# A fused mixing and MLP kernel on one Trainium2 core: LayerNorm 2 with tokens on partitions, first denominators on GpSimd, weights' low parts on VectorE, first fold behind the second slot

## The reference, cut to what matters

```python
def _layernorm(x, axis=-1, eps=1e-05):
    m = jnp.mean(x, axis=axis, keepdims=True)
    v = jnp.var(x, axis=axis, keepdims=True)
    return (x - m) / jnp.sqrt(v + eps)

# _wkv, a scan over the 128 tokens of a sequence, k = layernorm(x), v = ctx:
y = (A * p + E * vt) / (A * q + E)
return ((A2 * p + E2 * vt, A2 * q + E2, no2), y)

# ffn:
x = fwht(x * SU_ug) / SCALE
x_up = x @ W_up.T * (Wscale_ug[:INTER] * SCALE)
x_gate = x @ W_gate.T * (Wscale_ug[INTER:] * SCALE)
x = jax.nn.silu(x_gate) * x_up
x = fwht(x * SU_dp) / SCALE
x = x @ W_down.T * (Wscale_dp * SCALE)

# the whole:
x = x + jnp.tanh(g_xattn[0]) * wkv(w, u, _layernorm(x), ctx)
x = x + jnp.tanh(g_ffn[0]) * ffn(_layernorm(x), ...)
```

## Time and profile before

| | us |
|---|---|
| median of 3 runs | 110.72 |
| lowest and highest | 109.65 and 111.17 |
| the profiled execution | 110.77 |
| its span in the profile | 109.0 |

### The profile page before, as it was taken

The page is one execution under the profiler, slowest core; times in us unless marked ns, Lnnn a source line. Parts: engine busy times, 40 slices in busy tenths (PEclk is TensorE's granted clock), DMA queues, the critical chain, the costliest instruction groups (busy, mean ns, idle before and its releaser), DMA issues.

```text
span 109.0 us, 2031 instructions
## 1 busy us (share of the span) xinstructions
PE 102.0 (94%) x728; PEld 92.4 (85%) x728; DVE 69.7 (64%) x146; ACT 68.1 (63%) x153; POOL 61.2 (56%) x73
## 2 busy tenths in 40 slices
PE   6999999798999999978999999699999999999990
PEld 5787797477667999968999989699999999999980
DVE  0399987599999995798998259932277221134211
ACT  4099969889929899925337995555975532442400
POOL 7026995996995994149996246355207243234400
PEclk9999999999999999999999999999999999999998
DMA  1899999200000000000000000020000200000202
...
DMA packets 2893, 7.70 MB, mean 71 GB/s; under 512 B 321, under 2 KB 706, under 8 KB 2754
## 3 DMA queue, kind: packets, MB, share of 16 engines
...
HBM read 6.51 MB, written 1.05 MB: 69 GB/s over the span
## 4 chain that ended last, share of the span: by engine, by line
PE 59%; ACT 14%; DVE 14%; issue 9%; DVEq 0%; POOL 0%; ACTq 0%; POOLq 0%
PE UG L960 24%; PE VB L833 9%; PE OD L998 5%; PE VB L998 3%; PE FX L998 3%; PE KZ L998 3%; ACT L558 2%; PE FX L923 2%; ACT L561 2%; DVE DEN L720 2%; PE FX L877 2%; DVE SQ L664 2%; PE OD L890 2%; PE VB L890 2%; PE KZ L890 2%
## 5 line engine op out<-in xcount | busy, mean ns | idle before, releaser
L478 POOL TENSOR_TENSOR HL<-H,HH 128x256 fp32r<-128x256 f32 x32 | 26.0, 817 | 30.0 <-ACT HH L617 29.9
L810 DVE SCALAR_TENSOR_TENSOR H<-S,ALPHA,UG 128x256 f32<-128x256 f32 x32 | 15.0, 476 | 17.5 <-ACT S L626 17.4
L626 ACT ACTIVATE S<-UG,HI 128x256 f32<-128x256 f32 x32 | 14.8, 467 | 14.6 <-PE UG L960 14.6
L960 PE MATMUL UG<-FH,WTH 128*128 128x256 f32 x128 | 21.8, 293 | 0.8 <-DVE H L810 0.7
L617 ACT ACTIVATE HH<-H 128x256 fp32r<-128x256 f32 x32 | 13.2, 411 | 12.3 <-DVE H L810 12.2
L960 PE MATMUL UG<-FL,WTH 128*128 128x256 f32 x128 | 20.2, 280 | 0.5 <-DVE FL L781 0.5
L960 PE MATMUL UG<-FH,WTL 128*128 128x256 f32 x128 | 20.1, 279 | 0.0
L960 PEld LDWEIGHTS UG<-FH,WTH 128*128 128x128 f32 x128 | 17.6, 189 | 2.4 <-issue 1.2
L960 PEld LDWEIGHTS UG<-FL,WTH 128*128 128x128 f32 x128 | 17.2, 189 | 0.7 <-DVE FL L781 0.7
L960 PEld LDWEIGHTS UG<-FH,WTL 128*128 128x128 f32 x128 | 17.2, 188 | 0.0
L833 PE MATMUL VB<-ONES 128*128 128x256 f32 x32 | 9.9, 470 | 1.0 <-POOL ONES L432 1.0
...
## 6 DMA issues: line engine op xcount, KB each, us to landing
...
```

What stands on the lines that cost most here:

```text
L478: pool.tensor_tensor(HL[:, q % JT, 0:n], ring(H, q), HH[:, q % JT, 0:n].bitcast(F32), ALU.subtract).then_inc(h_lo, 1)
L626: act.activation(ring(S, q), gate_part(q), ACT.Silu, scale=VT[:, V_SGATE + j:V_SGATE + j + 1]).then_inc(silu_ready, 1)
L810: dve.scalar_tensor_tensor(out=ring(H, q), in0=ring(S, q), scalar=ALPHA[:, j:j + 1], in1=up_part(q), op0=ALU.mult, op1=ALU.mult).then_inc( ...
L960: return pe.matmul(dst.rearrange("p (g n) -> p g n", n=GT), w[:, m, j, t, :], f[:, chunks, t, :], start=start, stop=stop, skip_group_check ...
```

## The change

LayerNorm 2: `ones` now uses the squares as the stationary operand and one column of 1/C as the moving one, so the variances stand with tokens on partitions (128x2). `ve2` (VectorE, 128x2) adds eps, `rstd2` is a power of -0.5 on GpSimd (128x2), and the new TensorE stage `spread` transposes the broadcast result into VB. ScalarE copies FX to FN (`f_kept`), and `f_scaled` is a `tensor_tensor` of FN and VB. `root` is gone, as are the Ln and Exp of `rstd2` and GpSimd's `sum`.

Mixing, chunk 0: `mix_den` runs on GpSimd; for it, ScalarE makes a second exponential with another bias (`weighted`, tile EW). The load of the Ln and Exp table moves from `setup` to behind `center`.

Weights: `w_rest` is gone. `w_lo` 0 to 3 run on VectorE, from PSUM.

Order: the first fold `m` 0 moves from ahead of slot 0 to behind slot 1, `keys` 2 from there to behind slot 2, `warm_ug` is gone, `fwht`, `ones` and the exp blocks sit later, LAG is 7.

```diff
-LAG = 6
+LAG = 7
 PE_STAGES = {
-    -1: [("warm", 9), ("keys", 0), ("warm", 5), ("center", 0), ("w", 0), ("warm", 2), ("x_part", 0), ("w", 1), ("w_rest", 0), ("keys", 1), ("w", 2),
-        ("w_rest", 1), ("w", 3), ("y_part", 0), ("w_rest", 2), ("ones", 0), ("w_rest", 3), ("m", 0), ("warm_ug", 2), ("keys", 2)],
-    1: [("m", 1)],
-    2: [("m", 2)],
-    3: [("m", 3), ("fwht", 1)],
-    4: [("keys", 3), ("ones", 1)],
-    9: [("fwht", 2)],
-    12: [("ones", 2)],
-    17: [("fwht", 3)],
-    19: [("ones", 3)],
+    -1: [("warm", 9), ("keys", 0), ("warm", 5), ("center", 0), ("w", 0), ("warm", 2), ("x_part", 0), ("w", 1), ("y_part", 0), ("keys", 1),
+        ("ones", 0), ("w", 2), ("w", 3), ("spread", 0)],
+    1: [("m", 0)],
+    2: [("keys", 2), ("m", 1)],
+    3: [("m", 2)],
+    4: [("fwht", 1)],
+    5: [("m", 3), ("ones", 1)],
+    6: [("spread", 1)],
+    8: [("keys", 3)],
+    12: [("fwht", 2)],
+    13: [("ones", 2)],
+    14: [("spread", 2)],
+    19: [("fwht", 3)],
+    20: [("ones", 3)],
+    21: [("spread", 3)],
 }
 ACT_STAGES = {
+    -1: [("setup", 0), ("own", 0), ("signs", 0), ("decay", 0), ("keys", 0), ("weighted", 0), ("ratio", 0), ("center", 0), ("log_table", 0), ("recip", 0),
+        ("w_hi", 0), ("minus", 1), ("norm1", 1), ("w_hi", 1), ("square", 0), ("f_kept", 0), ("keys", 1), ("minus", 2), ("w_hi", 2), ("w_hi", 3), ("f_hi", 0), ("w_hi", 4), ("norm1", 2),
+        ("w_hi", 5), ("w_hi", 6), ("recip", 1), ("m_hi", 0), ("w_hi", 7), ("keys", 2)],
+    0: [("m_hi", 1), ("x_hi", 1)],
+    3: [("m_hi", 2)],
+    4: [("square", 1), ("f_kept", 1)],
+    5: [("m_hi", 3)],
+    6: [("f_hi", 1)],
+    8: [("exp_block", (("recip", 2), ("keys", 3)))],
+    9: [("x_hi", 2)],
+    12: [("square", 2), ("f_kept", 2)],
+    14: [("f_hi", 2), ("exp_block", (("recip", 3),))],
+    16: [("x_hi", 3)],
+    19: [("square", 3), ("f_kept", 3)],
+    21: [("f_hi", 3)],
 }
 DVE_STAGES = {
+    -1: [("stats1", 0), ("setup_rows", 0), ("norm1", 0), ("setup_shift", 0), ("stats1", 1), ("outs", 0), ("scan_a", 0),
+        ("av", 0), ("scan_av", 0), ("mix_num", 0), ("estimate", 0), ("newton", 0), ("w_lo", 0), ("w_lo", 1), ("stats1", 2), ("ve2", 0), ("stats1", 3),
+        ("f_scaled", 0), ("f_lo", 0), ("scan_a", 1), ("mix_den", 1), ("w_lo", 2), ("w_lo", 3), ("av", 1), ("m_lo", 0), ("scan_av", 1),
+        ("mix_num", 1), ("estimate", 1), ("newton", 1)],
+    0: [("x1", 1), ("m_lo", 1), ("x_lo", 1)],
+    2: [("scan_a", 2)],
+    3: [("m_lo", 2), ("mix_den", 2)],
+    4: [("ve2", 1)],
+    5: [("scan_av", 2), ("m_lo", 3)],
+    6: [("f_scaled", 1), ("f_lo", 1), ("mix_num", 2)],
+    8: [("estimate", 2), ("newton", 2), ("x1", 2)],
...
 }
 POOL_STAGES = {
+    -1: [("rstd1", 0), ("rstd1", 1), ("mix_den", 0), ("fly", 0), ("error", 0), ("fly", 1), ("fly", 2), ("fly", 3), ("rstd2", 0), ("fly", 6),
+        ("rstd1", 2), ("rstd1", 3), ("fly", 4), ("fly", 5), ("fly", 7), ("error", 1), ("w_lo", 4), ("w_lo", 5), ("av", 2)],
+    0: [("w_lo", 6)],
+    1: [("w_lo", 7)],
+    3: [("rstd2", 1)],
+    5: [("norm1", 3)],
+    7: [("error", 2), ("av", 3)],
...
 }
...
+                elif name == "mix_den":
+
+                    pool.wait_ge(weighted, 1)
+                    pool.wait_ge(scanned_a, 2)
+                    pool.tensor_tensor(lanes(DEN[:, 0, :, :, :]), lanes(EW[:, :, :, :]), lanes(states(SQ)), ALU.add).then_inc(den_ready, 1)
+                elif name == "rstd2":
+
+                    pool.wait_ge(half, 1)
+                    pool.wait_ge(ve2, g + 1)
+                    pool.tensor_tensor(RS2[:, :], VE2[:, :], NHALF[:, :], ALU.pow).then_inc(rstd2, 1)
...
-                elif name == "rstd2":
-
-                    act.wait_ge(v_full, g + 1)
-                    if g == 0:
-                        act.wait_ge(eps_set, 1)
-                    act.activation(RR[:, :], VB[:, 0:GT], ACT.Ln, bias=EPSC[:, 0:1]).then_inc(log_ready, 1)
-                    act.wait_ge(log_ready, g + 1)
+                elif name == "f_kept":
+
+                    act.wait_ge(f_full, g + 1)
                     if g:
-                        act.wait_ge(e_ready, 3 * g)
-                    act.activation(RR[:, :], RR[:, :], ACT.Exp, scale=-0.5).then_inc(rr_ready, 1)
+                        act.wait_ge(f_hi, CT * g)
+                        act.wait_ge(f_lo, g)
+                    act.activation(FN[:, :, :], FX[:, :].rearrange("p (t n) -> p t n", t=CT), ACT.Copy).then_inc(f_kept, 1)
...
+                elif name == "ve2":
+                    dve.wait_ge(v_full, g + 1)
+                    dve.tensor_scalar(VE2[:, :], VB[:, 0:GB], EPS * C, None, ALU.add).then_inc(ve2, 1)
                 elif name == "f_scaled":
-                    dve.wait_ge(e_ready, 3 * g + 3)
...
+                    dve.wait_ge(spread, g + 1)
+                    dve.wait_ge(f_kept, g + 1)
+                    for t in range(CT):
+                        dve.tensor_tensor(FN[:, t, :], FN[:, t, :], VB[:, GT:2 * GT], ALU.mult).then_inc(f_scaled, 1)
...
+                    for t in range(CT):
+                        pe.wait_ge(squared, t + 1 if g == 0 else CT + g)
+                        for b in range(GB):
+                            i = pe.matmul(VB[:, b:b + 1], FSQ[:, t, b * P:(b + 1) * P], ONES[:, 0:1], start=(t == b == 0), stop=(t == CT - 1), skip_group_check=True)
                     i.then_inc(v_full, 1)
+                elif name == "spread":
+
+                    pe.wait_ge(const_in, 16)
+                    pe.wait_ge(rstd2, g + 1)
+                    for b in range(GB):
+                        i = pe.matmul(VB[:, GT + b * P:GT + (b + 1) * P], RS2[:, b:b + 1].broadcast_to([P, P]), IDENT, is_transpose=True,
+                                      start=(b == 0), stop=(b == GB - 1), skip_group_check=True)
+                    i.then_inc(spread, 1)
```

More of the change, by code:

```diff
@@ L70 @@
+    0: [("m_hi", 1), ("x_hi", 1)],
[10 more added lines that the diff above has]
+    21: [("f_hi", 3)],
 }
 DVE_STAGES = {
-    -1: [("stats1", 0), ("setup_rows", 0), ("norm1", 0), ("setup_shift", 0), ("stats1", 1), ("outs", 0), ("scan_a", 0), ("mix_den", 0),
-        ("av", 0), ("scan_av", 0), ("mix_num", 0), ("estimate", 0), ("newton", 0), ("stats1", 2), ("stats1", 3),
-        ("scan_a", 1), ("root", 0), ("f_scaled", 0), ("mix_den", 1), ("f_lo", 0), ("m_lo", 0), ("av", 1), ("scan_av", 1), ("mix_num", 1),
-        ("estimate", 1), ("newton", 1), ("x1", 1)],
@@ new lines @@
+    0: [("x1", 1), ("m_lo", 1), ("x_lo", 1)],
[5 more added lines that the diff above has]
+    8: [("estimate", 2), ("newton", 2), ("x1", 2)],
+    9: [("x_lo", 2), ("scan_a", 3)],
+    11: [("mix_den", 3)],
+    12: [("ve2", 2)],
+    13: [("scan_av", 3)],
+    14: [("f_scaled", 2), ("f_lo", 2), ("mix_num", 3), ("estimate", 3), ("newton", 3)],
+    15: [("x1", 3)],
@@ L89 @@
+    16: [("x_lo", 3)],
+    19: [("ve2", 3)],
+    21: [("f_scaled", 3), ("f_lo", 3)],
 }
 POOL_STAGES = {
-    -1: [("rstd1", 0), ("rstd1", 1), ("fly", 0), ("fly", 1), ("fly", 2), ("error", 0), ("fly", 3), ("fly", 6), ("rstd1", 2), ("fly", 4), ("rstd1", 3),
-        ("fly", 5), ("fly", 7), ("w_lo", 4), ("error", 1), ("w_lo", 5), ("av", 2), ("norm1", 3)],
-    1: [("w_lo", 6)],
-    2: [("w_lo", 7)],
-    3: [("error", 2)],
-    5: [("av", 3)],
-    6: [("x1_first", 0)],
-    8: [("sum", 2)],
-    11: [("error", 3)],
@@ L100 @@
-    17: [("sum", 3)],
+    -1: [("rstd1", 0), ("rstd1", 1), ("mix_den", 0), ("fly", 0), ("error", 0), ("fly", 1), ("fly", 2), ("fly", 3), ("rstd2", 0), ("fly", 6),
[5 more added lines that the diff above has]
+    7: [("error", 2), ("av", 3)],
+    9: [("x1_first", 0)],
+    11: [("rstd2", 2)],
+    13: [("error", 3)],
+    18: [("rstd2", 3)],
@@ L135 @@
 W_HI, M_HI = (places(ACT_STAGES, n) for n in ("w_hi", "m_hi"))
-W_FULL, W_REST = (places(PE_STAGES, n) for n in ("w", "w_rest"))
+W_FULL = places(PE_STAGES, "w")
 X_HI = places(ACT_STAGES, "x_hi")
@@ L179, in build @@
         DN = sb("DN", [P, JT, C])
-        NI = sb("NI", [P, P], F32R)
         DB = sb("DB", [P, JT, C])
@@ L223, in build @@
             "signs", "wplus", "steps_r", "centers", "at_ready"))
[L225 to L226 removed]
+        filled, m_full, m_hi, w_full, w_hi = (sem(n) for n in (
+            "filled", "m_full", "m_hi", "w_full", "w_hi"))
         by_dve, by_pool, by_act = ({n: sem(f"{n}_{e}") for n in SHARED} for e in ("dve", "pool", "act"))
@@ L232, in build @@
         ln_ready, r0_ready, y0_ready, y_ready, y_first = (sem(n) for n in ("ln_ready", "r0_ready", "y0_ready", "y_ready", "y_first"))
-        x1_first, x1_ready, x_hi, f_full, squared, summed, v_full, log_ready, rr_ready = (sem(n) for n in (
-            "x1_first", "x1_ready", "x_hi", "f_full", "squared", "summed", "v_full", "log_ready", "rr_ready"))
-        e_ready, f_scaled, f_hi, f_lo = (sem(n) for n in ("e_ready", "f_scaled", "f_hi", "f_lo"))
+        x1_first, x1_ready, x_hi, f_full, squared, v_full, ve2, rstd2, spread = (sem(n) for n in (
```

(2 more changed lines are left out.)

132 lines of the change are left out of this document (35 added, 97 removed).

## The result

| | before | after |
|---|---|---|
| median, us | 110.24 | 113.73 |
| lowest and highest, us | 109.65 and 111.17 | 112.36 and 113.79 |
| the profiled execution, us | 110.77 | 113.79 |
| its span, us | 109.0 | 112.0 |
| granted clock over the span | 0.996 | 0.982 |

The ratio is 1.028 (1.017 to 1.039): the changed kernel is slower, by 3.0 us between the two profiled executions. Measured again beside fresh runs of before, it was 113.63 against 110.25, 1.027 (1.018 to 1.037). The forecast was 110.2, at most 112.5.

What follows compares the result with a forecast made beforehand. Bound by TensorE: slot 0's start, its work after that, and its waits. -2.6 + 2.4 + 1.35 - 2.3 + 0.6 = -0.55 us; forecast 110.2 us from 110.77 profiled, range 108.0 to 112.5.

Steps and rivals of the forecast that it cites:

- slot 0 and its FL earlier: Prologue to slot 0: slot 0's last products start at 23.3 instead of 25.89, -2.6 us (-2.05 to -3.05).
- the clock in slots 0 and 1: Rival, chance 0.14: TensorE's gaps ahead of slot 0 drop the clock for some 3.5 us, adding 1.75 us: 111.9.
- fold and keys moved: Behind slots 1 and 2: `m` 0 and `keys` 2, formerly inside the wait for `f_scaled`, are paid in full, +2.4 us.
- `ones` and `spread`, chunks 1 to 3: LayerNorm 2 on TensorE: 0.65 per `ones`, 0.25 per `spread`, less 1.34 for the old `ones`; +1.35 us (+0.15 to +2.05).
- waits ahead of slot 8 and behind it that go: Behind slot 8: TensorE's waits for `hidden`, `x_lo` 2, `x_hi` and `x_lo` 3 go, -2.3 us (-1.5 to -2.3).
- waits that come: Up to slot 8: TensorE waits for chunk 1's FH and FL behind VectorE's list, +0.6 us (0 to 2.5).
- The division: Chunk 0 in the prologue: nothing gained, 0.98 us lost in VectorE's wait; `newton` at 15.8 against 15.67.
- the blocking for `f_lo`: Ahead of slot 0's last products: `f_lo` beside GpSimd's work ends between 22.8 and 23.8; 1.56 us against 0.69 alone.
- The rival of VectorE's backlog: Slots 0 to 8, chance 0.13: VectorE operations lose time to GpSimd, 113.7 us at worst; sign, slot 8 after 46.5.

Runs made afterwards that it cites:

- `e_sum`: The changed kernel with GpSimd again adding the two tiles of squares for chunks 2 and 3, four loads instead of eight in `ones`; 116.5 us.
- `e_best`: `e_shift` with `estimate` and `newton` 2 moved behind slot 5 and chunk 2's `fwht`, square and sum one slot later; 111.7 us, 1.016 of before.
- `e_fold`: Before with `m` 0 behind slot 1, `keys` 2 behind slot 2, later folds one place on, six `warm_ug` ahead of slot 0; 114.92 us, 1.044 of before.
- `e_ln2`: Before with only the change's LayerNorm 2 (`ones`, `ve2`, `rstd2`, `spread`, `f_kept`), tiles at before's addresses; 111.98 us, 1.017 of before.
- `e_shift`: Before with chunk 3's `fwht` and all its later stages one slot later; 109.60 us, 0.988 of before.

## Why the prediction was wrong

The forecast was -0.55 us, and +3.0 came. The steps that failed are two terms that the prediction put at nothing: the fall of the clock as slot 0 starts, 1.5 us, and the pitch of TensorE's pairs, 2.0 us. By its own terms, counted in the two traces from one weight load to the next, a wait being what is over the pitch:

| term | forecast | measured |
|---|---|---|
| slot 0 and its FL earlier | -2.6 | -2.3 |
| the clock in slots 0 and 1 | none | +1.5 |
| fold and keys moved | +2.4 | +2.4 |
| `ones` and `spread`, chunks 1 to 3 | +1.35 | +1.4 |
| waits ahead of slot 8 and behind it that go | -2.3 | -3.5 |
| waits that come | +0.6 | +1.5 |
| pitch of the pairs | none | +2.0 |
| sum | -0.55 | +3.0 |

**The clock.** I had it as a rival at 0.14, with 1.75 us, and put it aside because "the longest gap is short". That step failed. The waits were 1.24 and 1.62 us long, the first as I had written (1.25), the second 0.7 longer (0.9), and in the two stretches of 3 us from 15 to 21 us TensorE was busy 2.12 and 2.74; then the granted clock went to the lower level, 1.2 of 2.4 GHz. From slot 0's first load (22.65) to the fold's (26.98) is 4.33 us, where 24 pairs at 119.8 ns are 2.88: +1.45. Filling both waits kept the clock at 1.00 in all four executions and took 1.0 off the median net, and executions without the fall are 1.2 to 1.4 faster. A single wait did it too: the products were idle 2.02 us in `e_sum` and 2.13 in `e_best` just before the clock fell, while 1.53 in `e_fold` and 1.43 in `e_ln2` left it at 1.00. What the prediction lacked was a reading of its own change as a whole: it took `w_rest` and `warm_ug` out for nothing and moved `m` 0 and `keys` 2 away. All four had helped to keep TensorE busy 10.96 of 11.60 us ahead of slot 0.

**The pitch.** Not in the prediction at all. I took products of one shape to cost the same in both kernels. The traces give +2.0: up to 58 us before ran mostly at 113.6 ns and after at 119.8 (some 200 pairs, 1.2 us), behind that at 117.8 and 119.8 (some 400 pairs, 0.8 us). The swapped layouts give 1.1 and 1.6; after's code at before's addresses has few stretches at 113.6. So the layout's share is shown, and why before's trace had the faster step for so long is not. The profile shows the pitch, but only where one looks at a stretch without waits and counts. The Trainium skill (TensorE: Matmul & The Clock Gate, Back-to-back issue gap) gives N / 2.4 + 2.5 ns for the gap of an isolated product at full clock, by which an estimate for 256 columns is 109.2 ns. The runs show 113.3 to 120.0 for load and product pairs.

**`ones`.** The mechanism was right (the loads set the price) and the size too low for one, though not for the sum. I took 0.65 between bounds of 0.25 and 0.88; from its first load to the next slot's it is 0.88 to 0.90 (41.24 to 42.12, 61.56 to 62.45), my upper bound, 0.11 for each of eight loads like `keys`': one column passing costs no less than 128. `spread` is cheaper, 0.17 to 0.21 of TensorE's time instead of 0.25. But before's `ones` cost more than the durations that I took off, counted in this way. The next slots in the trace of before (`ones` 1 and 2 start at 38.62 and 57.87):

```profile
39.39 0.65 PEld L960 LDWEIGHTS UG<-FH,WTH 128*128 128x128 f32 x4
...
58.20 0.64 PEld L960 LDWEIGHTS UG<-FH,WTH 128*128 128x128 f32 x4
```

0.77, 0.33 and 0.34 us, and each slot behind loses another 0.1 (0.65 and 0.64 instead of 0.54): 1.8, not 1.34. Together 2.67 + 0.55 - 1.77 = +1.45. That the sum came out as forecast is partly luck, since two misses cancel.

**The prologue.** `newton` at 15.40 (forecast 15.8), `y_part` 15.88 (16.25), the power's end 20.5 (20.45): right within 0.4, the late `ones` and the earlier division cancelling. The division gained 0.3 where I said nothing: `center` ran earlier than I had it, because its matmuls had ended at 10.80 and not at 11.2, and the table load moved up with it. `f_scaled` came at 21.68, not 20.87, and that is one row. The operation ahead of it on VectorE, `stats1` 3's last (L704, 128x2), took 1.13 us; it started 0.17 us after GpSimd's `fly` 6 and ended 0.04 after it. Alone it takes 0.17. I had named the blocking for `f_lo` only, and `f_lo` was free (0.69). Last, FL was in time for slot 0, so the old wait for it went, 0.77 us from load to load: -1.54 - 0.77 = -2.3.

**Moved work.** +2.4 stands, in after and in `e_fold`. The fold and `keys` 2 take the time they took before, at 27.10 and 30.25 us, with no wait of TensorE to hide them in.

**The waits that go.** All four of the earlier trace rows went, with a fifth of 0.28 at slot 16 and a small one ahead of slot 8: 3.5 us from load to load; what the loads still wait behind slot 8 are 0.19 and 0.30. The reason given is argued, not shown. In `e_ln2` the first two waits went with LayerNorm 2 alone, but there, as in after, TensorE comes to those places later than before did, so that a delay ahead of them is a rival. For the last two `e_shift` shows that one slot more is enough, without the rest of the change. So some of this gain could be had without it.

**The wait that comes.** From load to load it is 0.44 and 0.27 us up to slot 8, 0.21 ahead of `keys` 3, 0.25 and 0.37 at chunk 2's `ones` and `spread`: 1.5, and not 0.6. The place is another too: not VectorE's list ahead of FH and FL, but the squares that `ones` waits for and the round of three engines ahead of `spread`. I had costed that round at its durations only. With the waits that go it is -2.0 against a forecast of -1.7. The rival of VectorE's backlog isn't what happened: slot 8 starts after its limit of 46.5, at 46.57, but by the clock, the pitch and the waits above, and VectorE is busy 8.80 of 10 us there.

**The range.** Its upper end was 112.5, worked out from one rival at a time. The clock at its measured price gives 110.2 + 1.5 = 111.7, within the range; with the pitch it is 113.7, what was measured. The other terms were right in their sum to 0.2 us, though singly off by up to 1.2.
